# Fused attention and expert block on one core: row scatters one at a time, loads behind the keys' transpose, and a row ring of eight tiles

## What is computed

```python
x = x + tanh(g_xattn[0]) * attention(layernorm(x), ctx, ctx)   # 16 heads of 8; rope on keys and values
x = x + tanh(g_ffn[0])   * experts(layernorm(x))

# experts: 8 experts, the best 2 of each token
logits        = x @ gate_kernel                        # [tokens, 8]
w, chosen     = top_k(logits, 2);  w = softmax(w)
y[token]      = sum over its 2 experts n of  w_n * (silu(x @ w0[n]) * (x @ w1[n])) @ wo[n]
```

## Time and profile before

| | |
|---|---|
| median of 3 timed executions | 551.46 us (549.7 to 552.86) |
| the profiled execution, first to last instruction | 665.6 us |
| granted TensorE clock, mean of the profiled execution | 0.971 |
| PE busy, share of that span | 84% |
| ACT, DVE, POOL busy | 65%, 59%, 58% |
| attention stage in the profiled execution | to about 385 us |
| expert stage and results | from about 385 us to the end |

### The profile page before, as it was taken

The page is one execution under the profiler, slowest core; times in us unless marked ns, Lnnn a source line. Parts: engine busy times, 40 slices in busy tenths (PEclk is TensorE's granted clock), DMA queues, the critical chain, the costliest instruction groups (busy, mean ns, idle before and its releaser), DMA issues.

```text
span 665.6 us, 21070 instructions
## 1 busy us (share of the span) xinstructions
PE 561.5 (84%) x6123; PEld 468.0 (70%) x6124; DVE 393.9 (59%) x1418; ACT 431.8 (65%) x1090; POOL 384.0 (58%) x524
## 2 busy tenths in 40 slices
PE   8998898998989899899898779787778978888960
PEld 6886676776767677677776668676677868877860
DVE  6797787777778677677778643372133323223663
ACT  4897787887787788788777735344244546556540
POOL 3347756576575666657566466575545555545651
PEclk9999999999999999999999899897899999999995
DMA  3801111111111111111112112233222222225996
GB/s 91 240 20 57 42 42 52 36 55 40 48 44 36 56 40 48 48 33 58 41 55 63 33 50 73 64 98 101 85 64 80 77 74 76 76 68 174 270 272 206
DMA packets 64242, 52.98 MB, mean 80 GB/s; under 512 B 8607, under 2 KB 60064, under 8 KB 64176
## 3 DMA queue, kind: packets, MB, share of 16 engines
q1 hardware_dynamic: 46560, 30.79, 16.5%
q0 software_dynamic: 8448, 16.93, 7.7%
q10 hardware_dynamic: 9168, 4.46, 2.3%
HBM read 29.44 MB, written 23.22 MB: 79 GB/s over the span
## 4 chain that ended last, share of the span: by engine, by line
PE 51%; another core or an unknown queue 15%; issue 10%; ACT 8%; DVE 6%; ACTq 3%; DMA 2%; DVEq 2%; POOL 1%; SPq 1%; POOLq 0%
PE psK L583 10%; PE psH L603 8%; PE psH L483 5%; PE psH L489 4%; PE psG L498 4%; PE psH L498 3%; PE psK L471 3%; ACT wcur L757 3%; PE psO L619 2%; ACTq L319 2%; ACT ys L771 2%; PE psK L619 2%; ACT hs L764 2%; PE psO L518 2%
## 5 line engine op out<-in xcount | busy, mean ns | idle before, releaser
L1251 POOL DMA_INDIRECT results<-ys,zin x136 | 136.1, 1001 | 106.5 <-ACT ys L771 68.3
L603 PE MATMUL psH<-zT,wcur 128*128 128x128 f32 (+1 forms) x760 | 139.1, 333 | 20.1 <-ACT wcur L757 15.2
L1178 POOL DMA_INDIRECT lists<-zp,dest x128 | 129.6, 1012 | 34.8 <-issue 31.1
L603 PEld LDWEIGHTS psH<-zT,wcur 128*128 128x128 f32 x760 | 112.8, 195 | 34.4 <-ACT wcur L757 20.1
L1083 DVE TENSOR_TENSOR hm<-psH,hs 128x512 f32<-128x512 f32 x68 | 47.0, 692 | 121.0 <-remote 45.7
L977 DVE TENSOR_REDUCE mx<-psH 128x8 fp32r<-128x512 f32 x128 | 82.5, 686 | 43.4 <-PE psH L483 23.6
L696 ACT ACTIVATE ex<-psH,rs 128x512 f32<-128x512 f32 x128 | 86.8, 688 | 23.9 <-PE psH L489 16.3
L583 PEld LDWEIGHTS psK<-v,pT 128*64 128x64 f32 x2048 | 69.6, 137 | 37.1 <-issue 36.3
L583 PE MATMUL psK<-v,pT 128*64 128x64 f32 x2048 | 81.1, 226 | 9.0 <-issue 8.6
L757 ACT COPY wcur<-w 128x512 f32 x95 | 56.1, 619 | 15.2 <-issue 14.2
L747 ACT COPY v<-kvr 64x64 f32<-64x64 f32 x256 | 63.7, 249 | 2.2
(11 more groups left out here) (176 smaller groups left out, 1140.5 us busy)
## 6 DMA issues: line engine op xcount, KB each, us to landing
yy<-results SPq DMA_DIRECT2D x16, 512.0 KB
zin<-lists SPq DMA_DIRECT2D x41, 130.0 KB
out_dram<-x ACTq DMA_DIRECT2D x16, 256.0 KB
xring<-in_x_dram SPq DMA_DIRECT2D x31, 128.0 KB
cring<-in_ctx_dram SPq DMA_DIRECT2D x31, 128.0 KB
zin<-lists SPq DMA_DIRECT2D x54, 65.0 KB
results<-ys,zin POOLq DMA_INDIRECT x136
w<-in_L_ffn_w_kernel_dram SPq DMA_DIRECT2D x2, 1024.0 KB, 7.1
```

Source lines behind the costliest of these rows:

```text
L603: last = pe.matmul(bank[t.buf(2)][:, k * ET + c.start:k * ET + c.stop], wcur[:, t.buf(2), h, a, k * P:(k + 1) * P], zT[:, t.buf(2), c], st ...
L1178: nc.gpsimd.indirect_dma_start(lists, bass.IndirectOffsetOnAxis(ap=dest[:, t.buf(4), j:j + 1], axis=0), zp[:, t.buf(4), j, :], None).then_ ...
L1251: nc.gpsimd.indirect_dma_start(results, bass.IndirectOffsetOnAxis(ap=zin[:, t.buf(8), h, D:D + 1].bitcast(U32), axis=0), ys[:, t.buf(8), h ...
```

## The change

Five edits, all around the attention stage:

1. POOL no longer issues the two scatters of a tile one behind the other. The scatter of the first expert's rows goes ahead of `powers` and waits until the second scatter of the tile before it has landed; the scatter of the second expert's rows goes behind `powers` and `gaps` and waits until the first has landed.
2. The scatters of a tile come one step later (tile s - 6), and the attention loop of POOL runs one step longer. `tokens`, `counted` and the sums `before` go to the end of the step.
3. `zp`, `dest` and the semaphores `row_out` become rings of eight tiles; waits for a slot look eight tiles back.
4. SP's loads wait for the keys' transpose (`kT_ps`) of the tile four earlier, in place of `x1_done` and `ve_done` of the tile seven earlier.
5. The written-out steps ahead of the loop grow by three on DVE (`steady` 7 to 10) and ACT (11 to 14), so that a loop of eight steps begins at the same ring slot; POOL's `behind` is 6.

```diff
-                    if (t := ATT_POOL.at(s, -2)) and t.buf(4) == 3:
-                        tokens(t)
-                    if not static(s, NT - 1):
-                        powers(ATT_POOL.at(s, 0), ATT_POOL.at(s, 3))
-                    if (t := ATT_POOL.at(s, -2)) and t.buf(4) == 3:
-                        counted(t)
-                    if t := ATT_POOL.at(s, -5):
-                        scatter(t, range(2))
+                    if t := ATT_POOL.at(s, -6):
+                        if u := ATT_POOL.at(s, -7):
+                            wait_slot(pool, row_out, u, 32)
+                            carry(pool)
+                        scatter(t, (0,))
                     if static(s, NT):
                         powers(ATT_POOL.at(s, -1), None)
-                    if (t := ATT_POOL.at(s, -1)) and t.buf(4) == 3:
-                        wait_for(pool, chosen_done, t)
...
+                    elif not static(s, NT - 1):
+                        powers(ATT_POOL.at(s, 0), ATT_POOL.at(s, 3))
                     if (t := ATT_POOL.at(s, -1)) and t.buf(4) == 3:
...
+                    if t := ATT_POOL.at(s, -6):
+                        wait_slot(pool, row_out, t, 32, part=16)
+                        carry(pool)
+                        scatter(t, (1,))
+                    if (t := ATT_POOL.at(s, -2)) and t.buf(4) == 3 and not static(s, NT + 1):
+                        tokens(t)
+                        counted(t)
+                    if (t := ATT_POOL.at(s, -1)) and t.buf(4) == 3:
+                        wait_for(pool, chosen_done, t)
...
-                ATT_POOL.run(pool, attention_step, until=NT)
+                ATT_POOL.run(pool, attention_step, until=NT + 1)
...
-        zp = sb("zp", [P, 4, 2, ROW])
+        zp = sb("zp", [P, 8, 2, ROW])
-        dest = sb("dest", [P, 4, 2], U32)
+        dest = sb("dest", [P, 8, 2], U32)
-        row_out = [sem(f"row_out{i}") for i in range(4)]
+        row_out = [sem(f"row_out{i}") for i in range(8)]
...
+                def between_scatters(t):
+                    wait_for(sp, kT_ps, t, back=4)
...
                     for u in (0, 2):
-                        wait_for(sp, x1_done, Tile(4, turn, u - 7))
-                        carry(sp)
                         load_ready(Tile(4, turn, u))
-                        scattered(Tile(4, turn, u - 7))
+                        carry(sp)
+                        between_scatters(Tile(4, turn, u))
                         load(Tile(4, turn, u))
```

More of the change, by code:

```diff
@@ L107, in wait_for, with wait_slot @@
     eng.wait_ge(sem, v)
-def wait_slot(eng, sems, t, per, back=0):
+def wait_slot(eng, sems, t, per, back=0, part=None):
     n = len(sems)
     lap = t.k // n + (0 if t.turn is None else t.turn * (t.unroll // n))
-    v = per * (lap + 1 - back // n)
+    v = per * (lap - back // n) + (per if part is None else part)
     if isinstance(v, int) and v <= 0:
@@ L688, in normalised @@
                     wait_for(act, nm_done, t + (0 if t.buf(2) else 1))
-                    wait_slot(act, row_out, t, 32, back=4)
-                    nc.scalar.activation(zp[:, t.buf(4), :, 0:D], one(x1, t).unsqueeze(1).broadcast_to([P, 2, D]), ACT.Identity,
+                    wait_slot(act, row_out, t, 32, back=8)
+                    nc.scalar.activation(zp[:, t.buf(8), :, 0:D], one(x1, t).unsqueeze(1).broadcast_to([P, 2, D]), ACT.Identity,
                                          scale=rs[:, t.buf(4) // 2, 2 + t.buf(2):3 + t.buf(2)],
@@ L965, in row_weights @@
                     for i in (3, 2, 1, 0):
[L966 to L968 removed]
+                        wait_slot(dve, row_out, t + -i, 32, back=8)
+                    g = slice(t.buf(8) - 3, t.buf(8) + 1)
+                    nc.vector.tensor_scalar(zp[:, g, 0, D + 1], egap[:, :], -0.5, 0.5, ALU.mult, ALU.add).then_inc(weight_done, 2)
+                    nc.vector.tensor_scalar(zp[:, g, 1, D + 1], egap[:, :], 0.5, 0.5, ALU.mult, ALU.add).then_inc(weight_done, 2)
                 def destinations(t):
@@ L1184, in tokens @@
                     for i in (3, 2, 1, 0):
-                        wait_slot(pool, row_out, t + -i, 32, back=4)
+                        wait_slot(pool, row_out, t + -i, 32, back=8)
                     carry(pool)
-                    nc.gpsimd.tensor_copy(zp[:, :, :, D].bitcast(U32), src).then_inc(tok_done, 4)
+                    nc.gpsimd.tensor_copy(zp[:, t.buf(8) - 3:t.buf(8) + 1, :, D].bitcast(U32), src).then_inc(tok_done, 4)
                 def counted(t):
@@ L1241, in attention_step @@
                                                 rs[:, :, 2:4], ALU.mult).then_inc(gaps_done, 4)
+                    if t := ATT_POOL.at(s, -6):
[7 more added lines that the diff above has]
+                        wait_for(pool, chosen_done, t)
+                        for i in range(3):
+                            wait_for(pool, before_done, t, back=4 - i)
+                            nc.gpsimd.tensor_tensor(before[:, i + 1, :], before[:, i, :], chosen[:, i, :], ALU.add).then_inc(before_done, 1)
                 pool.wait_ge(zero_ready, 3)
-                ATT_POOL.run(pool, attention_step, until=NT)
+                ATT_POOL.run(pool, attention_step, until=NT + 1)
                 def experts_step(s):
```

21 lines of the change are left out of this document (9 added, 12 removed).

## The result

The changed kernel takes 681.16 us (median of four runs, 678.97 to 684.59); the kernel before, run beside it, 550.97 us (four runs, 549.70 to 552.86). The ratio is 1.237, with a 95% interval of 1.234 to 1.241: 130 us slower, where the prediction had 11 and its range ended at 579 us.

What follows compares the result with a forecast made beforehand. The prediction took PE's back-to-back work, 4.79 us per tile, as the bound; POOL's cycle exceeds it for 12.2 us, 11.1 net of cushion, other parts nothing: 551.5 + 11.1 = 562.6, given as 563 us, range 548 to 579.

Steps and rivals of the forecast that it cites:

- The late words: Profile before: PE's done signal reaches DVE late while POOL makes scatter descriptors, 1.18 us per attention tile; taken as recording only.
- the undisturbed run: Whole kernel rebuilt without late PE signals: attention 66 us and experts 56 us less than profiled, 544 us.
- Rival 2: Late PE signals are also in the timed run and the change removes them: faster, 547.5 us, chance 0.12.
- POOL becomes the bound: Attention steps 6 to 59: POOL's cycle 5.02 us per tile against PE's 4.79, 12.2 us, net 11.1.
- Rivals 1 and 4: 1: POOL keeps up with PE, 549 to 554 us, chance 0.27; 4: landings always over when POOL arrives, counted with 1.
- a plain link: POOL, scatter start to next scatter start: landing 2.08 us plus 0.30 us to start, 2.38 us, five in four tiles.
- The links with other work: POOL, four tiles: two scatter-to-scatter cycles with powers at 2.75 us, one with sums and kvr at 2.66 us.
- the upper bound: POOL: every scatter-to-scatter time 3.15 us, eight times over, 25.2 us for four tiles, 1.51 us per tile, 81 us.
- The transition: Attention to experts: scatters one step later delay the first result scatters, covered by ys's eight buffers for 23 us; nothing.
- Ring, loads, written-out steps: Ring of eight, SP's loads behind kT, and three steps moved on DVE and ACT: each predicted to change nothing.
- Rival 3: Loads moved among the scatters stretch landings, scatter-to-scatter time 2.9 us and more: 605 us, chance 0.07.
- What would show it: Changed kernel's profile: POOL idle near 1 us before L1182, ex awaiting rs, recorded tile period 5.0 to 5.6 us.

Runs made afterwards that it cites:

- Experiment 1: The kernel before, no edit, recorded a second time: 550.26 us, span 548.5 us.
- experiment 2: Changed kernel with both landing waits on POOL taken out: 552.33 us, ratio 1.0036 to the kernel before.
- Experiments 3 and 6: Changed kernel, both landing waits kept: 3 asks them of earlier scatters, 553.73 us; 6 puts the scatter's other four waits ahead of the landing wait, 659.35 us.
- experiment 5: Changed kernel with only the wait between tiles kept, the wait between a tile's two scatters taken out: 606.85 us.
- experiment 7: Changed kernel, both waits kept, with tokens and counted moved ahead of the first hold and the sums ahead of gaps and the second: 688.87 us.
- experiment 8: Changed kernel, both waits kept, with SP's loads waiting as in the kernel before: 679.63 us.

## Why the prediction was wrong in size

**The late words.** I put them down to recording. Experiment 1 shows that they came with one execution. What I drew from it held: the undisturbed run has none, its tiles take 4.8 to 4.9 us, and the sum had to be made against that. But the reading that PE's word is late because POOL makes descriptors falls: in experiment 1 a scatter lies across the same place, and DVE starts 0.15 us after PE's end. The rule on trace records that I cited from the Trainium skill does not make the delay by itself: the same kernel, recorded a second time, shows none. Rival 2 falls with it.

**POOL becomes the bound.** Right, and it is all of the slowdown: without holds it is gone (experiment 2). Rivals 1 and 4, in which POOL keeps up, fall with it. What failed is the size of the cost.

**The link: the step that failed.** I took 2.38 us for a plain link, 2.08 for a landing and 0.30 for the next start; it measured 3.447. Put into the same sum, eight links of 3.447 us make 27.58 us for four tiles, 8.42 over PE's 19.16, 2.105 per tile; times 54 steps, less the 1.05 us of cushion, 112.6 us. Measured: 112.4. The link was measured in the kernel that it explains, so this tests the frame of the sum alone: POOL's chain sets the tile. That it fits to 0.2 us is in part luck, since the tiles without holds took 4.87 us in the mean of the last 56 and not 4.79, and with that the sum gives 108. The frame was right and one term of it, the link, was not:

- *The restart* was the larger miss, 0.30 against 0.96 us in the mean of the 89 links (for instance a landing at 109.99 + 2.48 = 112.47 us, the next scatter at 113.42; and 205.79 to 206.79). The 0.30 us is the gap between two scatters that stand in the queue together. A held scatter did not have it in any of the 89 links. The trace of before showed the price where a scatter came out of a wait: in its chain ACT's `ys` ended at 643.15 us and the result scatter that needed it started at 643.96, 0.81 us later (start us, us, what):

```profile
642.90 0.25 ACT ys L771
...
643.96 0.58 POOL results L1251
```

  Experiments 3 and 6 show the restart apart: nearly free when it lies beside other work, 0.25 us of it saved by order, 0.78 us left.
- *The landing* took 2.49 us in the mean, against 2.08. I took the last result scatter, alone at the end of the kernel. In the changed kernel that one again takes 2.09 us (chain of waits), while a row scatter takes 2.3 at the least and 2.4 in the median (below, min/median/max of all landings in the row lists, a few loads of SP's among them), and 2.80 in the mean beside loads (experiment 5). Why a row scatter takes 0.2 us more even without loads beside it, and in the hole between the stages too, is not shown.

```profile
664.66 2.09 DMA results<-ys,zin
```
```profile
DMA to landing us min/median/max: 2.3/2.4/5.2
```

The estimate of 2.15 us from the Trainium skill, page "DMA: Bandwidth & Descriptors", section "Anatomy of one DMA — SWDGE (gpsimd) path", was below the least of this view as well; that a fixed part is paid with every scatter, as I read the page, is what happened.

**The links with other work.** 2.75 us with the powers and 2.66 with the sums were sums of POOL's own work; such links took 203.22 - 199.96 = 3.26 and 186.15 - 182.91 = 3.24 us, since the landing and the restart are longer than that work. For a link that awaits nothing 2.75 was a fair price: with the powers it took 208.08 - 205.42 = 2.66 us in experiment 5. All eight links were bounded by the landing. I had written that case down as the upper bound, 3.15 us eight times over and 81 us, from the earlier trace rows, a row in which an instruction had come out of a wait for a scatter, and kept a third of the way to it. The right mechanism was in the bound and not in the value that I took, and even the bound was 0.30 us a link too low; its row ended in a copy, not in another scatter.

**The transition**, priced at nothing. The cover that I named, the eight buffers of `ys`, stands before the result scatters. What came late first was something else in POOL's queue, the last sums behind held scatters: a wait of 13.7 us on PE, of 17.6 us that the expert stage is longer.

**PE's wait for the sums** was not in the prediction. It is the same lag seen at a second place (experiment 7), not a second cost.

**Ring, loads, written-out steps:** nothing, as predicted, but for the ring's 0.2%.

**Rival 3** had the right mechanism, a longer link, with the moved loads as its cause and 2.9 us as its size, and a chance of 0.07. Its cause is wrong as the main one: with the loads moved back the time is the same (experiment 8). Landings with loads beside them did take 0.40 us more in the mean, but they are 19 of 89, which is 0.09 us in the mean link.

**What would show it.** POOL idle before L1182 with the DMA as releaser: yes, 112.8 / 60 = 1.9 us each and not 1. No more long idleness before `ve`: yes, 5.3 us in three waits for DVE, where it was 86.5 us in 31. ACT's `ex` waiting for `rs`: yes. A recorded tile period of 5.0 to 5.6 us and a profiled span that gets shorter while the time gets longer: no, the period was 6.89 us and the span grew; both rested on the late words.

## What to carry to other kernels

A chain of transfers that each await the one before costs, per link, the landing plus a full restart of the issuing engine (here 2.49 and 0.96 us): take the restart from a row in which the engine comes out of a wait, never from the gap between two transfers that were queued together. If it is enough that a transfer comes after those some way back, ask for the landing two or three transfers back: here that was 553.73 us against 681.16, with the same waits on POOL. And follow an engine that falls behind to the end of its stage, where everything queued behind it is paid for once more.

## What the runs showed of the hardware

- An indirect DMA on POOL started 0.94 to 1.28 us, 0.96 in the mean of 89, behind a landing that it awaited; about 0.52 us of that has no record of any kind, and stays when the landing wait is the last thing ahead of it (206.06 to 206.58 us and 210.01 to 210.53 us in the chains above).
- The scatter's start to its landing is 2.3 us at best: about 1.0 us of work on POOL, and, in the medians of the packet and semaphore records of the changed kernel's 128 row scatters, the first packet 0.58 us behind that, the last packet's end 0.93 us and the last landing 1.34 us behind it. Moving the bytes is 0.35 us of it.
- Row scatters with packets of SP's loads between the end of their work on POOL and their landing landed after 2.80 us in the mean (19 of them), the others after 2.40 us (70).
- The recorded execution shown first was 117 us longer than a second one of the same kernel (665.6 against 548.5 us), with DVE idle behind words of PE that came late. What set it off that once, no run here shows.
- PE's granted clock was 1.00, the 2.4 GHz level, in the stretch where PE was busy throughout, and 0.91 in the mean from 110 to 420 us, where PE was idle for a fifth of the time: at the lower level, 1.2 GHz, for 54.6 of these 310 us by the trace's clock records, which show no third level.
